# A product-interaction MLP on one core: the first two k tiles taken tile by tile, a new order of the work, and a clear on GpSimd after the gathers

## The reference

```python
sparse_embed = emb_tables[field_idx[None, :], x_sparse]      # (1024, 26, 64)
z = sparse_embed.reshape(B, N_FIELDS * K)                    # (1024, 1664)
gram = jnp.einsum('bik,bjk->bij', sparse_embed, sparse_embed)
inner = gram[:, iu, ju]                                      # (1024, 325), i < j
dnn_in = jnp.concatenate([x_dense, z, inner], axis=-1)       # (1024, 2002)
h = jax.nn.relu(dnn_in @ w1 + b1)                            # w1: (2002, 2002)
out = jax.nn.sigmoid(h @ w2 + b2)                            # (1024, 1)
```

## Time and profile before

| | |
|---|---|
| median of 3 runs | 450.62 us (450.54 to 452.58) |
| span of the profiled execution | 584.9 us |
| its own time | the page gives the span alone |
| busy: TensorE matmul | 436.1 us (75%) |
| busy: VectorE, ScalarE, GpSimd | 316.2, 274.3, 215.9 us |
| mean granted TensorE clock | 0.872 |

### The profile page before, as it was taken

One profiled execution on the slowest core, in us unless ns is written; L12 is line 12 of the kernel. 1 busy time (PEld: TensorE's weight loads), 2 busy tenths in 40 slices (PEclk: granted clock), 3 DMA queues, 4 the chain that ended last, 5 costly groups with the idle time before them and its releaser, 6 DMA issues.

```text
span 584.9 us, 6070 instructions
## 1 busy us (share of the span) xinstructions
PE 436.1 (75%) x2011; PEld 355.6 (61%) x2011; DVE 316.2 (54%) x670; ACT 274.3 (47%) x443; POOL 215.9 (37%) x215
## 2 busy tenths in 40 slices
PE   7814040999787899445999932059989999999997
PEld 7613030777675777334887721047867888887885
DVE  4510010565638698302679830049886478989542
ACT  2400020383689867315986630029543368864330
POOL 6777772477723437770005777700000000000000
PEclk9967575899999999755999975568989999999999
DMA  7643351569634857441356863312666373465730
GB/s 232 154 71 62 26 98 12 155 160 277 189 78 117 201 156 226 85 61 34 113 156 206 214 153 26 62 36 62 152 206 219 102 244 106 141 193 196 258 90 0
DMA packets 29455, 77.96 MB, mean 133 GB/s; under 512 B 8480, under 2 KB 8488, under 8 KB 29424
## 3 DMA queue, kind: packets, MB, share of 16 engines
q1 hardware_dynamic: 22768, 70.75, 38.8%
q0 software_dynamic: 6656, 6.83, 11.4%
HBM read 77.55 MB, written 0.00 MB: 133 GB/s over the span
## 4 chain that ended last, share of the span: by engine, by line
PE 42%; another core or an unknown queue 18%; ACT 15%; issue 12%; DVE 9%; DMA 2%; SPq 1%; POOL 1%; DVEq 0%; ACTq 0%
PE ps L562 13%; PE ps L574 12%; PE ps L564 12%; ACT w_hi L627 4%; DVE w_lo L733 3%; ACT gram L662 3%; DVE weighed L837 2%; PE ps L522 2%; ACT pair_u L648 2%; ACT pair_v L651 2%; PE ps L508 2%; DMA w_raw<-in_L_rec_w_dram 1%; ACT pair_v L650 1%; SPq L392 1%
## 5 line engine op out<-in xcount | busy, mean ns | idle before, releaser
L451 POOL DMA_INDIRECT z<-in_L_rec_emb_tables_dram,idx x208 | 214.9, 1033 | 162.6 <-PE ps L508 99.4
L562 PE MATMUL ps<-w_hi,x_hi 128*128 128x502 f32 (+1 forms) x512 | 212.5, 415 | 73.2 <-issue 46.5
L564 PE MATMUL ps<-w_lo,x_hi 128*128 128x502 f32 (+1 forms) x480 | 194.0, 404 | 4.6 <-issue 4.6
L733 DVE TENSOR_TENSOR w_lo<-w_raw,w_hi 128x1002 fp32r<-128x1002 f32 x120 | 141.2, 1200 | 100.8 <-ACT w_hi L627 51.6
L627 ACT CAST w_hi<-w_raw 128x1002 fp32r<-128x1002 f32 x128 | 128.7, 1033 | 83.6 <-remote 27.7
L562 PEld LDWEIGHTS ps<-w_hi,x_hi 128*128 128x128 f32 x512 | 101.1, 197 | 102.9 <-issue 55.6
L574 PE MATMUL ps<-w_hi,x_lo 128*128 128x502 f32 (+1 forms) x480 | 142.8, 403 | 4.0 <-issue 3.1
L564 PEld LDWEIGHTS ps<-w_lo,x_hi 128*128 128x128 f32 x480 | 95.1, 198 | 21.4 <-issue 4.2
L574 PEld LDWEIGHTS ps<-w_hi,x_lo 128*128 128x128 f32 x480 | 92.8, 196 | 23.9 <-issue 4.3
L635 ACT CAST x_hi<-ps 128x256 fp32r<-128x256 f32 (+2 forms) x36 | 16.2, 472 | 121.6 <-PE ps L508 62.2
L662 ACT COPY gram<-ps 32x104 f32<-32x104 f32 x160 | 39.7, 248 | 54.3 <-remote 32.7
(11 more groups left out here) (46 smaller groups left out, 184.4 us busy)
## 6 DMA issues: line engine op xcount, KB each, us to landing
w_raw<-in_L_rec_w_dram SPq DMA_DIRECT2D x112, 501.0 KB
w_raw<-in_L_rec_w_dram SPq DMA_DIRECT2D x24, 250.5 KB
w_raw<-in_L_rec_w_dram SPq DMA_DIRECT2D x8, 438.4 KB
z<-in_L_rec_emb_tables_dram,idx POOLq DMA_INDIRECT x208
w_raw<-in_L_rec_w_dram SPq DMA_DIRECT2D x24, 62.6 KB
w2b<-in_L_rec_w_dram SPq DMA_DIRECT2D x1, 501.0 KB
w2b<-in_L_rec_w_dram SPq DMA_DIRECT2D x1, 500.0 KB
w_raw<-in_L_rec_w_dram SPq DMA_DIRECT2D x8, 50.9 KB
```

The source lines that it names most:

```text
L451: pool.indirect_dma_start(out=z[:, t % 2, K * f:K * (f + 1)], out_offset=None, in_=emb_rows, in_offset=bass.IndirectOffsetOnAxis(ap=idx[:, ...
L562: nc.tensor.matmul(into(c, t), hi, of_w(w_hi, c, k), start=first, stop=False)
L564: nc.tensor.matmul(into(c, t), hi, of_w(w_lo, c, k), start=False, stop=False)
L733: nc.vector.tensor_tensor(low, raw(n)[at, :], high, ALU.subtract).then_inc(w_lo_done, 1)
```

## The change

Four edits:

1. **Tile by tile.** For k tiles 0 and 1 of pair 0, the transposes of tile 0 and tile 1 are events of their own (`ALONE = 2`), and turns 0 to 3 do all matmuls of tile 0 first, then those of tile 1. Every turn still has 12 matmuls.
2. **A new `PLAN`**, and `WARM` is empty: the 21 spare matmuls placed by W (not the 36 at the start) go. Weight pieces 2 and 3 are split one turn earlier (`FIRST` in `ahead`), the clearing of `pair_u` and `pair_v` moves ahead of the first split on VectorE, and the computing of the later row numbers (`make_rows`) behind turn 0's work.
3. **A clear and a wait on GpSimd.** Behind the two gathers of a tile's k tile, GpSimd writes zeros into one column (128 x 1) of a new tensor `rest`, and waits for that write before it goes on. It does so for k tiles 4 to 12 of pair 0 and for all of tiles 2 to 7: 9 x 2 + 13 x 6 = 96 times.
4. Nothing is taken from the reference's work; the gathers, the loads and the matmuls on data are as many as before.

```diff
-    JOINT = [[(0, 1), (1, 1), (2, 1), (3, 1), (4, 1), (5, 1), (6, 1), (7, 1), (8, 1), (9, 1), (10, 1), (11, 1), (12, 1)], [(0, 2), (2, 2), (4, 2), (6, 2), (8, 2), (10, 2), (12, 1)]]
+    ALONE = 2
+    HASTY = 4
+    BOTH = tuple(range(GROUP))
+    JOINT = [[(k, 1, (b,)) for k in range(ALONE) for b in BOTH] + [(k, 1, BOTH) for k in range(ALONE, FP)],
+             [(0, 2, BOTH), (2, 2, BOTH), (4, 2, BOTH), (6, 2, BOTH), (8, 2, BOTH), (10, 2, BOTH), (12, 1, BOTH)]]
...
-        ('J', 1): [25.0, 26.0, 28.8, 30.5, 32.5, 35.7, 37.5],
+        ('J', 1): [25.2, 26.3, 29.2, 30.1, 32.8, 36.1, 38.2],
...
-        ('R', 5): [69.4],
-        ('X', 5): [69.9],
+        ('R', 5): [68.8],
+        ('X', 5): [70.1],
...
-    WARM = [(2.9, 6), (5.2, 1), (33.3, 4), (34.4, 4), (39.7, 6)]
+    WARM = []
...
-            return [m for m in range(2, PIECES) if max(PIECE[m][0] - LEAD, turns_before(m) - 1, 0) == u]
+            return [m for m in range(2, PIECES) if max(PIECE[m][0] - LEAD, turns_before(m) - 1, FIRST) == u]
...
+                if t >= GROUP or k >= HASTY:
+                    n = FP * t + k
+                    nc.gpsimd.memset(rest[:, n:n + 1], 0.0).then_inc(rested, 1)
+                    rests.append(n)
+                    pool.wait_ge(rested, len(rests))
...
+            later = [second_alone(k) for k in range(ALONE)]
             for u in range(FIRST, TURNS):
-                if u >= 0:
+                if 0 <= u < HALVES * ALONE:
+                    if u % HALVES == 0:
+                        multiply(u, 0)
+                        transpose_z(second_alone(u // HALVES))
+                        multiply(u + 1, 0)
+                    multiply(u, 1)
+                elif u >= 0:
                     multiply(u)
                 for kind, t, q in between(u):
-                    PARTS[kind](t, q)
+                    if (kind, t, q) not in later:
+                        PARTS[kind](t, q)
```

More of the change, by code:

```diff
@@ L162, in product_interaction_mlp_kernel @@
+        ('R', 7): [101.2],
         ('X', 7): [102.1],
     }
[L164 removed]
+    WARM = []
     KINDS = "JTOGRXW"
@@ L219, in slices_of @@
         if kind == "J":
-            first, n = JOINT[t][q]
-            return [(GROUP * t + b, k) for b in range(GROUP) for k in range(first, first + n)]
+            first, n, of = JOINT[t][q]
+            return [(GROUP * t + b, k) for b in of for k in range(first, first + n)]
         first, n = BATCHES[q]
@@ L226, in slices_event @@
         if t < GROUP * EARLY_PAIRS:
-            return next(("J", t // GROUP, q) for q, (first, n) in enumerate(JOINT[t // GROUP]) if first <= k < first + n)
+            return next(("J", t // GROUP, q) for q, (first, n, of) in enumerate(JOINT[t // GROUP])
+                        if first <= k < first + n and t % GROUP in of)
         return next(("T", t, q) for q, (first, n) in enumerate(BATCHES) if first <= k < first + n)
@@ L502, in transpose_z @@
                 if kind == "J":
-                    pe.wait_ge(gathered_j[q], 16 * 2 * GROUP * sum(js[q][1] for js in JOINT[:t + 1]))
+                    pe.wait_ge(gathered_j[q], 16 * 2 * sum(js[q][1] * len(js[q][2]) for js in JOINT[:t + 1]))
                 else:
@@ L577, in low_part @@
                     return last
-                pe.wait_ge(w_hi_done, FIRST_LOAD[FIRST_PIECE[m] + len(ks)])
-                pe.wait_ge(w_lo_done, FIRST_LOAD[FIRST_PIECE[m] + len(ks)])
-                if LAST_OF[sums_of(m)[0]] == m or LAST_OF[sums_of(m)[-1]] == m:
+                if only is None or only == tiles[0]:
+                    pe.wait_ge(w_hi_done, FIRST_LOAD[FIRST_PIECE[m] + len(ks)])
+                    pe.wait_ge(w_lo_done, FIRST_LOAD[FIRST_PIECE[m] + len(ks)])
+                if only is not None:
+                    for c in cs:
+                        high_parts(c, only, ks[0])
+                        last = low_part(c, only, ks[0])
+                    if only != tiles[-1]:
+                        return
+                elif LAST_OF[sums_of(m)[0]] == m or LAST_OF[sums_of(m)[-1]] == m:
                     for c in cs:
@@ L633, in high_z @@
                 (t, k), n = slices[0], slices[-1][1] - slices[0][1] + 1
-                b = GROUP if kind == "J" else 1
+                b = len(slices) // n
                 nc.scalar.copy(x_hi[:, t % XS:t % XS + b, k:k + n, :],
@@ L722, in _ @@
             nc.vector.memset(w2b[:, 1, 0:2], 0.0).then_inc(w2_zero, 1)
+            for pairs in (pair_u, pair_v):
+                pads = pairs[:].bitcast(fp32).rearrange("p a s (r k) b -> p (a s) r (k b)", r=2)
+                last = nc.vector.memset(pads[:, :, :, 2 * FP:], 0.0)
+            last.then_inc(pad_zero, 1)
             def split_piece(m):
```

87 lines of the change are left out of this document (44 added, 43 removed).

## The result

The changed kernel takes 461.12 us (median of 4 runs, 453.99 to 465.86), the kernel before 450.58 us (median of 4). The ratio is **1.016, with a 95% interval of 1.009 to 1.023**: slower by 1.6%, where 1.0% faster was predicted. The profiled execution of after took 453.99 us, with a span of 452.2.

What follows compares the result with a forecast made beforehand. TensorE was taken as the bound outside three stretches where it almost stops, seen only in the profiled execution. 450.6 - 2.3 - 1.9 - 0.9 - 1.4 - 1.7 + 3.3 = 445.7, say 446 us, 1.0% faster; range 439 to 457.

Steps and rivals of the forecast that it cites:

- the room of the gathers: At pair 1's fifth transposes: the 92nd gather's data there at 127.9, TensorE at 134.9, so 7.0 us ahead.
- The clear and its wait: On GpSimd, 0.16 us each; 38 stand ahead of pair 1's fifth transposes, making them 3.3 us late: +3.3.
- the first hole: Stretch from 29 to 106 us of the profiled execution of before where TensorE almost stops; 62.7 us taken out.
- a level arrival would have left small waits in the runs: Argument against gathers at pace 1.37, whose data would arrive level with TensorE at pair 1's fifth transposes.
- The gathers had no room: Chance 0.20: gathers arrive level with TensorE at pair 1's fifth transposes, lateness 10.3 eats gains of 8.2: 452.7 us.
- The clear drains GpSimd: Chance 0.26: each clear waits until gathers are wholly done, 0.56 us each, late at pair 1's transposes: 460.9 us.
- The clears cost nothing that is seen: Chance 0.14: clears fall into the 0.30 us gaps between gathers on GpSimd, lateness goes to 0: 442.4 us.
- The holes are in the runs too: Chance 0.06: runs hold some 8 us of TensorE nearly stopped beside unbroken gathers; clears end this: about 438 us.
- Tile by tile: At the start: first transpose at 11.76 for 12.96, turn 2 at 18.5 to 19 for 21.29: -2.3 us.
- The spare matmuls: Leaving them out saves 1.9 us in turn 3, 0.9 in turns 33 and 34, 1.4 at the last six; clock unaffected.
- The tails: Tiles 5 and 3 get more distance; half of their waits of 2.34 and 1.03 us saved: -1.7 us.
- What would show it: Signs: first transpose about 11.8, turn 2 before 19.5, gather pair with clear 2.5 to 3.2 us, tails' waits under 1.

Runs made afterwards that it cites:

- the joint kernel: Changed kernel without clears, with k tiles 0 and 1 of pair 0 taken for both tiles at once as before; ratio 1.005, median 453.12 us.

## Why the prediction was wrong

**The step that failed is the room of the gathers**, in "The clear and its wait": "I take the middle, 1.31, there at 127.9, 7.0 ahead." The sum there was late by 6.1 + 4.2 - 7.0 = 3.3. The runs show, term by term:

- the clears: 3.7 us, not 6.1 (38 x 0.10, not 38 x 0.16);
- TensorE earlier at turn 26: 4.4 us, as taken (4.2);
- the room in before: 1.5 us, not 7.0. Its pace was (127.16 - 3.8) / 92 = 1.34 us a gather, and the transposes came at 131.7, not at 134.9, since the two traces of before stand 65.9 us apart there, and the first hole was taken out with 62.7;
- a term that I did not have: the gathers of the new order last 6.4 us longer by the 92nd, and 7.0 with clears.

3.7 + 4.4 - 1.5 + 6.4 = 13.0 us late in place of 3.3. With it the sum is 450.6 - 8.2 + 13.0 = 455.4 us; the profiled execution took 453.99, 1.016 x 450.6 is 457.8, and the median of all four runs was 461.1. Without clears it is 451.7, and the measured ratio of 1.002 gives 451.5. That late gathers eat the gains is shown, by the 16 gathers fewer from the other side. That the corrected sum comes so near is in part luck: the 8.2 of gains hold a term with the wrong sign (below), and the loss is not made at the one place at which the sum has it. TensorE waits 2.27 us at pair 1's second transposes and 3.8 us in pair 0, of which the prediction said "No wait of TensorE for `z` before pair 1":

```profile
24.80 0.44 PE L524 MATMUL ps<-ident,z 128*128 128x128 f32 x2 [1.45 <-DMA z<-in_L_rec_emb_tables_dram,idx]
...
141.28 0.62 PE L524 MATMUL ps<-ident,z 128*128 128x128 f32 x4
```

At the fifth transposes the changed kernel does not wait at all: they start at 141.28, 3.5 us behind the issue of the 92nd gather. Without clears they wait 2.71 there. So the gathers lack room in pair 0 already, and that they meet TensorE first at pair 1's fifth transposes was a second thing that the prediction had wrong.

**The argument behind that step was bad too.** "143 would mean a wait of 8 us in the runs, for which 451 against 450.6 leaves no room" is true, but "a level arrival would have left small waits in the runs" is not: a kernel can have its gathers arrive 1.5 us ahead with no wait at all, and that is what before has. The absence of waits says that the room is not below zero, and nothing more; the middle of a range was no reading of it. The range had a slip too: an arrival at 134.9 means a pace of (134.9 - 3.88 - 3.46) / 92 = 1.39, not 1.37, and from the right middle the room would have been 5.7.

**The rivals.** "The gathers had no room" named the mechanism and gave 452.7; it is where the changed kernel without clears stands. "The clear drains GpSimd" gave the right sign for a wrong reason: the gap is 0.38, not 0.86, and that its 460.9 us lies beside the median of all runs, 461.1, is luck. What the rule on complete instructions in the Trainium skill ("GPSIMD Engine Reference", section "2.1 Instruction dispatch") would make of it, 0.56 us, is not borne out: the clear starts at the end of the gather's record. "The clears cost nothing that is seen" holds only, more or less, for clears without waits; with the waits they cost 1.4%. "The holes are in the runs too" is wrong: before without holes has a span of 450.1. My reading that the runs are the profiled execution less its holes (451) was right.

**The other terms.** *Tile by tile*, -2.3: turn 2 came at 19.0 (20.2 in before profiled again, so 1.2 earlier), the first transpose at 11.91 as said, but the joint kernel is at turn 26 as early. *The spare matmuls*, -4.2 in sum: wrong in sign for the kernel before, where they are worth 0.8%, 3.7 us; the step is what was said of the clock, "so I put nothing on it". *The tails*, -1.7: before waits 3.3 us there, the changed kernel 1.9, a gain of 1.4. Not counted at all: the products' wait for `pair_v` ahead of turn 25, 2.96 us in before, is 1.25 in the new order, and the stretch at the lower clock behind it is gone. From the start of turn 24 to that of turn 26 before takes 13.75 us and the kernel without clears 10.73: these 3.0 are most of the 4.4 us at turn 26 that I had given to the start and the spare matmuls, a right number for partly wrong reasons.

**What would show it.** The first transpose, turn 2 and the tails' waits (0.8 at most) came as said. A wait of a few us at pair 1's transposes was right (2.3; the wait of 3.0 is tile 4's), no wait before them was wrong. The pair with its clear was to take 2.5 to 3.2 us, and takes 2.57 where nothing lengthens it (33.86 to 36.43), so the mark was met and yet the kernel is slower: the mark, 3.3 us or more, was set too high, since it rested on the 7.0 us of room.

## What to carry to other kernels

Before a producer's stream is slowed or its consumer sped up, measure by how much the data is ahead at each place where they meet; "no wait" does not say that. A gain ahead of such a meeting point is worth at most the room there, and leaving out part of the producer's work shows in one run whether the rest of the change is any good. A row of another stage is no pace for this one: the first 92 gathers took 1.34 us each in before, 1.41 in the new order with nothing changed in them, and 1.46 with the clears. And look at what a gather starts under (below).

## What the runs showed of the hardware

**A wait can cost more than its length.** The kernel before, at the wait ahead of turn 25:

```profile
93.94 1.27 PE L522 MATMUL ps<-pair_v,pair_u 128*128 128x128 f32 x8 [2.96 <-ACT pair_v L651]
95.02 0.72 PE L562 MATMUL ps<-w_hi,x_hi 128*128 128x502 f32 x1
95.54 0.62 PE L564 MATMUL ps<-w_lo,x_hi 128*128 128x502 f32 x1
95.95 0.62 PE L574 MATMUL ps<-w_hi,x_lo 128*128 128x502 f32 x1
...
98.57 0.39 PE L562 MATMUL ps<-w_hi,x_hi 128*128 128x500 f32 x1
98.80 0.39 PE L564 MATMUL ps<-w_lo,x_hi 128*128 128x500 f32 x1
```

Behind the wait the matmuls follow each other at 0.42 us, and from 98.6 on at 0.23 again. The granted clock of the two stretches (the figure behind the five engines' busy times, which are PE, PEld, DVE, ACT and POOL) is 0.50, the level of 1.2 GHz, and 1.00, that of 2.4:

```profile
94.80:98.10 3.30, 3.30 (x11) 2.69 (x11) 0.27 (x1) 3.16 (x10) 2.69 (x3) 0.50 0.36 32
98.20:101.00 2.80, 2.11 (x14) 1.69 (x12) 1.29 (x2) 2.71 (x6) 2.19 (x3) 1.00 0.44 72
```

Not every such wait is followed by this: in the kernel without clears the clock is 1.00 from 136 to 140 us and from 164 to 172, behind waits of 2.71 and 3.29. In the changed kernel it is 0.83 between 120 and 150 us, with two of the waits above in or ahead of it; in the kernel without clears 0.94:

```profile
120.00:150.00 30.00, 26.16 (x112) 21.81 (x112) 19.55 (x48) 22.10 (x44) 24.22 (x31) 0.83 0.66 157
```

```profile
120.00:150.00 30.00, 25.79 (x125) 21.02 (x126) 21.30 (x54) 21.15 (x44) 23.96 (x20) 0.94 0.72 172
```

PE looks as busy in both, with 13 matmuls fewer in the first. In the table the time at full clock is within 2 us of 440 for eleven of the kernels that do all the work, while their medians run from 449 to 455.

**The gathers' length follows what VectorE does when they start.** The 0.94 us is a floor; beside VectorE's splits of the weights a gather lasts up to 1.9 as a rule, and single ones longer, 2.85 in the kernel without clears. That kernel, GpSimd and VectorE:

```profile
131.49 2.32 DVE L768 TENSOR_TENSOR w_lo<-w_raw,w_hi 128x1002 fp32r<-128x1002 f32 x2 [0.78 <-ACT w_hi L658]
131.83 1.68 POOL L461 DMA_INDIRECT z<-in_L_rec_emb_tables_dram,idx  x1 [0.31 <-issue]
133.81 0.94 POOL L461 DMA_INDIRECT z<-in_L_rec_emb_tables_dram,idx  x1 [0.30 <-issue]
```

```profile
21.10 0.94 POOL L461 DMA_INDIRECT z<-in_L_rec_emb_tables_dram,idx  x1 [0.30 <-issue]
21.62 1.20 DVE L768 TENSOR_TENSOR w_lo<-w_raw,w_hi 128x1002 fp32r<-128x1002 f32 x1 [0.21 <-ACT w_hi L658]
...
28.18 0.67 DVE L854 TENSOR_TENSOR zpart<-ps,zpart 128x500 f32<-128x500 f32 x1
28.27 0.94 POOL L461 DMA_INDIRECT z<-in_L_rec_emb_tables_dram,idx  x1 [0.30 <-issue]
```

The gather of 131.83 starts while a split's subtract (1.2 us; two are merged in the row) still has 0.85 us to go, and lasts 1.68. The one of 21.10 starts ahead of such a subtract and lasts 0.94, though the subtract begins in it. The one of 28.27 starts under a subtract of another kind, which reads one of its inputs from PSUM, and lasts 0.94 too. By their records, the 20 traces of this case have 964 gathers that start while a split's subtract runs, with more than 0.13 us left of it: 97% of them last 0.94 us, plus what is left of the subtract, less 0.13, to within 0.03 us. The gathers that start ahead of a subtract have a median of 0.94, and of the 126 that start under a subtract of `zpart` none is over 0.96. So a gather stands until a running subtract of this kind is over; the traces show no other pattern for these 97%. It does not go the other way: the subtracts that begin in a gather last 1.20 us like the others.

This accounts for most of the missing term. Of the first 92 gathers 20 start under such a subtract in before and 23 in the kernel without clears, and they are 7.9 and 13.0 us over 0.944 each, of 8.7 and 15.1 in all: 5.1 of the 6.4 us. The number of splits is the same; when the gathers start against them is not. The first 92 gathers have 8.7 to 11.3 us of excess in the four kernels with the whole old order and 13.2 to 17.8 in those with the new row of pair 0, one with two clears (10.9) aside. What in the new order brings the starts under the subtracts stays open.

In the Trainium skill, "SBUF — State Buffer", section "SBUF: two separate sides", a VectorE operation with two inputs in SBUF can lock GpSimd out of a shared port, against an operation of GpSimd that reads SBUF, and whichever of the two starts first has the port until it is done. The traces agree for the gather that starts second, and not for the subtract that does (1.20 us either way). That descriptors wait, the section says of another kind of VectorE operation; that the port is what holds the gathers is not shown here.
